# Right operands' sums spread over five value heads, x blocks loaded early, narrow products first

## The reference, cut to what matters

```
Q = x @ Wq ; K = ctx @ Wk ; V = ctx @ Wv          # x: 2 x 2048 x 512, ctx: 2 x 77 x 384, 8 heads of 512
attn = softmax(Q @ K.T / sqrt(512))               # per head, over the 77 keys
out  = concat(attn @ V) @ Wo + x                  # Wo: 4096 x 512
out  = (out - mean) * rsqrt(var + eps) * gamma + beta
```

## Time and profile before

| | us |
|---|---|
| median of 3 runs | 377.33 (377.31 to 377.4) |
| the profiled execution | 378.28 |
| its span, first to last instruction | 376.5 |
| PE busy (2328 matmuls) | 348.5 |
| DVE busy | 295.5 |
| ACT busy | 244.9 |
| POOL busy | 232.1 |

### The profile page before, as it was taken

The page is one execution under the profiler, slowest core; times in us unless marked ns, Lnnn a source line. Parts: engine busy times, 40 slices in busy tenths (PEclk is TensorE's granted clock), DMA queues, the critical chain, the costliest instruction groups (busy, mean ns, idle before and its releaser), DMA issues. The chain is left out here.

```text
span 376.5 us, 7129 instructions
## 1 busy us (share of the span) xinstructions
PE 348.5 (93%) x2328; PEld 316.1 (84%) x2328; DVE 295.5 (78%) x557; ACT 244.9 (65%) x794; POOL 232.1 (62%) x232
## 2 busy tenths in 40 slices
PE   9999999946699963999999999999999999999994
PEld 6999999835588853998998988988989989989984
DVE  2269996799954761689898898898898889889896
ACT  2277556626274561797787697696797697687461
POOL 2046430984274395359878868867877867966233
PEclk9999999996999998699999999999999999999999
DMA  7997678652644301602154143134143234223003
GB/s 243 423 422 286 246 285 310 241 186 86 201 154 166 121 7 52 235 3 96 74 167 141 41 157 139 57 140 141 56 141 141 71 127 143 81 113 109 34 30 111
DMA packets 21348, 56.25 MB, mean 149 GB/s; under 512 B 2560, under 2 KB 4928, under 8 KB 19392
## 3 DMA queue, kind: packets, MB, share of 16 engines
q1 hardware_dynamic: 20448, 54.81, 40.5%
q10 hardware_dynamic: 864, 1.00, 0.9%
HBM read 46.98 MB, written 8.39 MB: 147 GB/s over the span
## 5 line engine op out<-in xcount | busy, mean ns | idle before, releaser
L776 PE MATMUL pair<-vw_hi,pt_hi 128*128 128x512 f32 x155 | 62.2, 401 | 0.0
L776 PE MATMUL pair<-vw_hi,pt_lo 128*128 128x512 f32 x155 | 60.9, 393 | 0.0
L776 PE MATMUL pair<-vw_lo,pt_hi 128*128 128x512 f32 x155 | 60.6, 391 | 0.0
L1466 POOL TENSOR_TENSOR out_sb<-centred,beta_sb 128x512 f32<-128x512 f32 x30 | 38.7, 1290 | 29.0 <-ACT centred L987 29.0
L701 PE MATMUL pair<-a_hi,xo_hi 128*128 128x304 f32 x128 | 40.7, 318 | 9.6 <-DVE u_w L1214 6.1
L942 ACT ACTIVATE prob<-c,neg_max 128x77 f32<-128x77 f32 x128 | 43.9, 346 | 0.0
L1511 POOL TENSOR_TENSOR xo_lo<-x_sum,xo_hi 128x512 fp32r<-128x512 f32 x32 | 41.4, 1298 | 0.0
L701 PE MATMUL pair<-a_lo,xo_hi 128*128 128x304 f32 x128 | 39.3, 307 | 0.0
L701 PE MATMUL pair<-a_hi,xo_lo 128*128 128x304 f32 x128 | 39.3, 307 | 0.0
L980 ACT ACTIVATE pt_hi<-pair 128x640 fp32r<-128x640 f32 x32 | 22.5, 703 | 22.8 <-PE pair L763 22.8
L1299 DVE TENSOR_TENSOR pair<-pair,x_in 128x512 f32<-128x512 f32 x31 | 21.7, 699 | 18.6 <-PE pair L776 16.7
(11 more groups left out here) (141 smaller groups left out, 1066.5 us busy)
## 6 DMA issues: line engine op xcount, KB each, us to landing
w_out<-wo SPq DMA_DIRECT2D x8, 1024.0 KB, 4.8
xt_in<-x_tiles SPq DMA_DIRECT2D x16, 512.0 KB, 4.0
x_in<-x_rows SPq DMA_DIRECT2D x16, 512.0 KB, 4.8
out<-out_sb SPq DMA_DIRECT2D x31, 256.0 KB, 2.2
w_out<-wq_t SPq DMA_DIRECT2D x7, 1024.0 KB, 7.6
w_proj<-wv SPq DMA_DIRECT2D x8, 768.0 KB, 4.9
w_proj<-wk SPq DMA_DIRECT2D x6, 768.0 KB, 9.4
w_out<-wq_t SPq DMA_DIRECT2D x2, 512.0 KB, 7.9
```

Of the source, the lines that this page charges most:

```text
L776: mm = pe.matmul(ps_out[:, i % 2, 0:s.model], ps[:, j, :], v[:, j, b, :], start=(j == 0 and n == 0), stop=(j == s.key_t - 1 and n == len(p ...
L1466: pool.tensor_tensor(out_sb[i % OUT_RING][:, :], centred[i % 2][:, :], beta_sb[:, :], ALU.add)\
```

## The change

- The sums are made in another order (T1, T3, T2, T4, first all of batch 0, then all of batch 1), with two of the four places in PSUM: `sum_z` in `pairs[1]`, `sum_w` in `pairs[3]`. To free these, the value projections' two halves now lie in the two banks of `pairs[0]`, and the main product and the strips have one bank each, in `pairs[2]`. So head h's main product waits for DVE's lo part of head h - 1, and the strips for ACT's copy of head h - 1.
- DVE, ACT: head 8 has T1, T3, T2 of batch 0, head 9 their lo parts and T4, head 10 T4's lo part and T1, T3, T2 of batch 1, head 11 lo parts and T4, head 12 T4's lo part.
- PE: `value_strips(u)` stands ahead of `value_product(u)`. ACT takes the strips ahead of the main product, too.
- `load_xt(0)` is issued in head 10, `load_xt(1)` in head 11.
- The lo part of Wo of head 14 is POOL's instead of DVE's.
- In the main stage ACT's `split_rest` stands ahead of `round_sums(1)`; DVE's `split_rest` stands behind all of the first pair's combining.
- `bias_rows` (the mask's row) and `clear_pad` are earlier.

```diff
-    RESTS_OF_VECTOR = (USES - 2, USES - 1)
+    RESTS_OF_VECTOR = (USES - 1,)
-    T_ORDER = (T1, T2, T3, T4)
-    T_PARTS = [(n, b) for n in T_ORDER for b in range(s.batches)]
+    T_ORDER = (T1, T3, T2, T4)
+    T_PARTS = [(n, b) for b in range(s.batches) for n in T_ORDER]
-        ps_vw = [ps_outp[0][:, n, 0:s.model] for n in range(2)]
-        ps_strips = [ps_outp[1][:, n, 0:P] for n in range(2)]
+        ps_vw, ps_strips = pairs[2][:, 0, 0:s.model], pairs[2][:, 1, 0:P]
+        sum_z, sum_w = pairs[1][:, :, 0:s.kept_half], pairs[3][:, :, 0:s.kept_half]
         def right_steps(b):
-            x, y, z, w = t_tmp[b]
+            x, y, z, w = t_sb[b][:, :, :], t_sb[s.batches][:, :, :], sum_z, sum_w
             return [(z, hi[0][1], lo[0][1], ALU.add), (w, z, hi[0][0], ALU.subtract), (x, w, lo[0][0], ALU.subtract),
-                    (w, hi[1][1], lo[1][1], ALU.add), (y, w, x, ALU.subtract),
-                    (z, w, z, ALU.subtract),
-                    (w, hi[1][0], y, ALU.subtract), (x, w, lo[1][0], ALU.add)]
+                    (y, hi[1][1], lo[1][1], ALU.add), (w, y, z, ALU.subtract),
+                    (z, y, x, ALU.subtract),
+                    (w, hi[1][0], z, ALU.subtract), (x, w, lo[1][0], ALU.add)]
+        def t_sum(n, b):
+            return {T1: t_sb[b][:, :, :], T3: sum_w, T2: sum_z, T4: t_sb[b][:, :, :]}[n]
# SP
-            for c in range(XT_RING):
-                load_xt(c)
+                if H + 2 <= u < H + 2 + XT_RING:
+                    load_xt(u - H - 2)
# PE, value_product and value_strips
-                elif h >= 2:
-                    pe.wait_ge(dve_vw_lo, 2 * (h - 1))
+                else:
+                    pe.wait_ge(dve_vw_lo, 2 * h)
-                if h >= 2:
-                    pe.wait_ge(act_strip, h - 1)
+                if h == 0:
+                    pe.wait_ge(dve_a_lo, 2 * H)
+                else:
+                    pe.wait_ge(act_strip, h)
-                    value_product(u)
-                    value_strips(u)
+                    if u == USES - 1:
+                        open_bank_a()
+                    value_strips(u)
+                    value_product(u)
# ACT
-                if u == H + 1:
-                    for part in T_PARTS[:4]:
-                        round_t(*part)
+                if H < u <= H + 4:
+                    b = (u - H - 1) // 2
+                    if (u - H) % 2:
+                        round_t(T3, b)
+                        round_t(T2, b)
...
+                elif u < USES - 1:
+                    take_strips(u - H)
+                    split_vw(u - H)
+                    if u < H + 4:
+                        round_t(T4 if (u - H) % 2 else T1, (u - H) // 2)
+                else:
                     seed(0)
-                split_vw(u - H)
-                take_strips(u - H)
...
+                    take_strips(u - H)
+                    round_blocks(1)
+                    split_vw(u - H)
             copy_s1(0)
+            split_rest()
             round_sums(1)
-            split_rest()
# DVE
-                if u == H:
-                    right_sum(T1, 0)
+                if u == H + 4:
+                    split_t(T4, 1)
+                elif u < H + 4:
+                    b = (u - H) // 2
+                    if (u - H) % 2:
+                        split_t(T1, b)
+                        split_t(T3, b)
+                        split_t(T2, b)
+                    else:
+                        if b:
+                            split_t(T4, b - 1)
+                        right_sum(T1, b)
                 if u + 1 < USES and by_vector(u + 1):
                     split_w_out(u + 1)
-                if u == USES - 1:
-                    bias_rows()
                 split_vw(u - H)
-                if u == H:
-                    right_sum(T1, 1)
-                    for n in (T2, T3):
-                        for b in range(s.batches):
-                            right_sum(n, b)
...
+                if u < H + 4:
+                    if (u - H) % 2:
+                        right_sum(T4, b)
+                    else:
+                        right_sum(T3, b)
+                        right_sum(T2, b)
+                elif u == H + 4:
+                    bias_rows()
...
-            add_u2(0)
-            split_rest(0)
-            add_w2(0)
+            combine_first(0)
             max_c11(0)
             combine_c22(0)
             combine_c12(0)
             combine_c21(0)
-            split_rest(1)
+            for b in range(s.batches):
+                split_rest(b)
```

More of the change, by code:

```diff
@@ L132, in build @@
             lt("gap1", [P, 256])
-            mask_bias = lt("mask_bias", [P, s.batches, s.half])
-            lt("gap3", [P, P])
+            lt("gap3", [P, s.row + P])
             x_in = [lt(f"x_in{n}", [P, CHUNK, s.model]) for n in range(X_RING)]
@@ L146, in build @@
         with ExitStack() as spare:
-            t_tmp3 = spare.enter_context(nc.sbuf_tensor("t_tmp3", [P, KT, s.kept_half], F32))
+            mask_bias = spare.enter_context(nc.sbuf_tensor("mask_bias", [P, s.batches, s.half], F32))
         rest = [sb(f"rest{n}", [P, 2, s.toks]) for n in range(2)]
@@ L203, in build @@
             with ExitStack() as parts:
-                t_tmp4 = [parts.enter_context(nc.sbuf_tensor(f"t_tmp4_{n}", [P, KT, s.kept_half], F32)) for n in range(3)]
+                second_keys = parts.enter_context(nc.sbuf_tensor("second_keys", [P, s.kept_row], F32))
             wo_lo_late = et("wo_lo_late", [P, s.model_t, s.dim_t, P], F32R)
@@ L311, in second, with keys_at, values_at, whole_proj @@
             return pair[:, :, toks_of(u):2 * toks_of(u)]
+        def keys_at(half):
+            return ps_proj[half][:, :, 0:s.toks]
+        def values_at(half):
+            return pairs[0][:, half, 0:2 * s.toks].rearrange("p (m k) -> p m k", m=2)
+        def whole_proj(u, half):
+            return values_at(half) if u >= H else keys_at(half)[:, :, 0:s.toks if u == 0 else s.kept_toks]
         def ctx_of(u):
@@ L580, in short_product, with full_product @@
                 return mm
-            def full_product(pair, bank, w, moving, m, tiles):
-                toks = moving.shape[2]
+            def full_product(to, w, moving, m, tiles):
                 for k in range(tiles):
-                    mm = pe.matmul(pair[:, bank, 0:toks], w[:, m, k, :], moving[:, k, 0:toks],
+                    mm = pe.matmul(to[:, m % 2, :], w[:, m, k, :], moving[:, k, :],
                                    start=(k == 0), stop=(k == tiles - 1))
@@ L677, in value_product @@
                     for n, (low, w) in enumerate(passes):
-                        mm = pe.matmul(ps_vw[h % 2], values(u, k, low), w[:, k, :], start=(k == 0 and n == 0),
+                        mm = pe.matmul(ps_vw, values(u, k, low), w[:, k, :], start=(k == 0 and n == 0),
                                        stop=(k == s.dim_t - 1 and n == len(passes) - 1))
@@ L1123, in split_kv @@
                     if whole(u):
-                        dve.scalar_tensor_tensor(out=tiles[:, :, toks:2 * toks], in0=first(ps_proj[half], u),
+                        dve.scalar_tensor_tensor(out=tiles[:, :, toks:2 * toks], in0=whole_proj(u, half),
                                                  scalar=kv_scale[u], in1=tiles[:, :, 0:toks].bitcast(F32),
```

89 lines of the change are left out of this document (35 added, 54 removed).

## The result

| | us |
|---|---|
| before, 4 runs | 377.37 (377.31 to 378.49) |
| after, 4 runs | 371.38 (370.9 to 373.41) |
| ratio | 0.9845 [0.9804, 0.9885] |
| profiled execution of after, its span | 370.9, 369.1 |

A forecast was written before the change was run, and what follows sets the result against it. PE, busy 93% of the span, was taken as the bound, with waits to remove. Second pair 7.6 us earlier less 1.6 for the clock, 5.9 taken: 372.4 profiled, median 0.95 below, 371.4; eight in ten 365.5 to 376.

The forecast's parts named there:

- Head 8's wait: On PE, head 8's strips, now leading, wait for POOL's `v_rest` behind Wo's lo part: 2.3 us lost.
- ScalarE's waits for T4: In the value heads, ScalarE's in-order queue waits at L948 for DVE's T4 sum, twice about 5 us.
- The waits at projections 12 and 14: PE waits 2.5 us at each for DVE's lo part, late because ScalarE's rounding waited for T4.
- End of the heads: Value heads end at 134.3 us, gaining 0.9, after 14.3 us of PE waits in ten pieces.
- Strips of heads 11 and 13: On PE, these narrow products were to wait 1.2 us in head 11 and 1.4 us in head 13.
- Rival 3: Heads 11 to 15: the clock falls among small waits and stays down, giving 379.3 us; chance 0.11.
- Sums into PSUM: DVE sums with both inputs in SBUF still take turns with POOL: five turns a batch instead of twelve.
- Rivals 1 and 2: DVE sums: PSUM results free them, 365.7 us, chance 0.14; or all are held and long, 373.7 to 378.1, chance 0.11.
- The strips' chain: Head 14's copy at 128.6, sixteen DMAs end at 141.2, second pair starts at 146.4, 7.6 us earlier.
- The mis-sized term: Behind the second pair's start, all 5.5 us of half clock instead of 2.3: 1.6 us more.
- The sum: At the third pair's first product: 7.6 earlier less 1.6 for the clock, net 6.0 us, taken as 5.9.
- the removal of the 3.5 us wait: Ahead of the score products: with x there early, PE's 3.5 us wait for POOL's lo part goes.

The follow-up runs named there:

- e1: Changed kernel with ScalarE's rounding of T1 and T4 (`round_t`) one head later; 362.98 us, ratio 0.9618 to the kernel before.
- e7: Changed kernel with SP loading both x blocks behind head 13's strips; 376.73 us, ratio 0.9993 to the kernel before.
- e6: Changed kernel with ScalarE copying head 14's strips ahead of the first x block's rounding; 369.06 us, ratio 0.9795 to the kernel before.
- b2: Kernel before with VectorE's two `split_rest` behind all of the first pair's combining, ScalarE's order kept; 376.66 us, ratio 0.9977.
- e3: Changed kernel with both x blocks loaded late, behind the loop over the heads; 372.21 us, ratio 0.9855 to the kernel before.
- b1: Kernel before with the two x blocks loaded inside the loop over the heads, at heads 13 and 14; 375.3 us, ratio 0.9941.
- e2: Changed kernel with the strips' rows split later on ScalarE and VectorE; 370.14 us, ratio 0.9811 to the kernel before.
- e4: Changed kernel with the main product ahead of the narrow ones, on TensorE and ScalarE; 369.6 us, ratio 0.9801 to the kernel before.
- e8: Changed kernel with VectorE making the mask's row (`bias_rows`) in head 15 again, instead of head 12; 373.25 us, ratio 0.9866 to the kernel before.
- c2: Changed kernel with later `round_t` of T1 and T4, late strips' split, third x block ahead of head 15's strips, and main product first; 356.21 us, ratio 0.9462.
- e5: Changed kernel with head 8's `v_rest` ahead of Wo's lo part on GpSimd; 368.95 us, ratio 0.9784 to the kernel before.
- c1: Changed kernel with later `round_t` of T1 and T4, head 8's `v_rest` first, late strips' split, third x block ahead of head 15's strips; 354.88 us, ratio 0.9402.

## Why the prediction was right, step by step

- **Heads 8 to 15.** Head 8's wait: 2.3 predicted, 1.97 measured. ScalarE's waits for T4: about 5 twice, measured 4.95 and 5.30; e1 shows that they are the cause. The waits at projections 12 and 14 (the expectation of e1 calls the first projection 11): 2.5 and 2.5, measured 2.27 and 2.25. End of the heads: 134.3, measured 134.04, of which 0.53 is the start; the gain was to be 0.9 and is 0.6. That the end fits is in part luck: the 14.3 us of losses laid out were all waits, the measured ones are 10.7 us of waits and some 3.3 us by the clock at projections 12 and 14 (from their start to the next product 4.99 and 4.95 us, against 3.32 at the upper clock from 102.34).
- **The small waits were partly the wrong ones.** Strips of heads 11 and 13 were to wait 1.2 and 1.4 us; they do not, because the projection ahead took 1.7 us longer by the clock. That is Rival 3's mechanism at two places, and one sign that the prediction named for being wrong, a clock below 0.9 in heads 11 to 15, did come (0.65 and 0.66 in these two stretches, 0.92 as the mean from 91.21 to 134.04). In head 11 it cost nothing: in e7 the clock stayed up at the same place, PE waited 0.79 us for `v_rest` and 1.71 us for the lo part instead, and the main product began 6.97 us behind the projection, against 6.96 in after. In head 13 `v_rest` is there at 116.62 and the strips begin at 117.75, so about 1 us was lost, an estimate from these two rows. It did not last: Rival 3, a clock that stays down through the heads, fell.
- **Sums into PSUM.** Held or not was decided by the inputs, as assumed:

```profile
69.84 0.80 DVE L1211 TENSOR_TENSOR pair<-pair,a_hi 128x608 f32<-128x608 f32 x1
...
77.91 2.30 DVE L1211 TENSOR_TENSOR pair<-t_sb 128x608 f32<-128x608 f32 x1
...
92.16 2.94 DVE L1211 TENSOR_TENSOR pair<-a_hi,a_lo 128x608 f32<-128x608 f32 x1
```

```profile
70.00 4.73 POOL L1552 TENSOR_TENSOR wo_lo_odd<-w_out,w_out_hi 128x1024 fp32r<-128x1024 f32 x2
...
89.24 5.21 POOL L1552 TENSOR_TENSOR wo_lo_odd<-w_out,w_out_hi 128x1024 fp32r<-128x1024 f32 x2 [5.90 <-ACT w_out_hi L891]
```

  With one input in PSUM the sum takes 0.80 us beside POOL's lo part; with both in SBUF and the result in PSUM (the second and third row) it takes 2.30 and 2.94. The rule of the Trainium skill, page "SBUF — State Buffer", section "SBUF: two separate sides", that the lock goes by "two SBUF inputs", agrees. Rivals 1 and 2 both fall.
- **The strips' chain.** Head 14's copy at 128.6, measured 127.67; moves end at 141.2, measured 140.49; second pair at 146.4, measured 145.59, 8.37 earlier than before where 7.6 were predicted. e6 and e7 move this chain both ways.
- **The mis-sized term** is the clock behind the wait: 1.6 predicted. From the second pair's start to the mark it is 11.48 us before and 12.58 after, so 1.1; b2 gives the same 1.07. The 2.3 us behind 153.96 were right, but the second pair of after does not run 5.5 us at the lower level: its matmuls come every 0.25 us from 145.59 to 150.06 only and then every 0.14, and in half-microsecond steps the clock is at 0.50 from 143.5 on, 2 us ahead of the pair's start. So about 4.5 us of the lower level lie behind the start instead of 5.5.
- **The sum.** 8.37 - 1.10 = 7.27, less 0.53 of the start is 6.7, where 6.0 stood; the medians differ by 6.0. The profiled executions differ by 7.38, since that of before lay 0.9 above its median and that of after 0.5 below. That the median was hit to 0.02 us is luck.
- **A reading to set right.** The prediction calls the clock about half behind each wait of the earlier trace rows. Its first two rows, 0.66 and 0.64, are means over a part at 0.50 and a part at 1.00 (behind the 8.8 us wait it is 0.50 until 91.5 and 1.00 from 92.0). And there was one more such stretch, behind the 3.5 us wait for POOL: in half-microsecond steps the clock is 0.50 from 139.5 to 142.5. It was hidden by the 6.1 us wait that followed, so the sum does not change.
- **What I credited wrongly.** I let the early x load carry the removal of the 3.5 us wait. e3 shows that it isn't needed: in the changed kernel SP reaches the old place of the loads at 119.02 instead of 124.81, as head 12's strips are copied at 112.3 instead of 117.16. Only where SP gets there late (e7, b1) does the order count. b1 and b2 alone bring 2.1 and some 0.8 us. No run has the spread sums, the new banks or the earlier mask's row alone on the kernel before, so how the remaining 3 us are shared stays open.

## What to carry to other kernels

An engine that works in order makes every wait in its queue a wait of all that stands behind: look at the longest waits of the engines that are not the bottleneck, and ask what is behind them. Here moving four roundings by one head each was worth 8.4 us, more than the whole change. And where work is dealt out to remove a long stall, lay the queues out by hand from the trace's durations. It told the gain of the combined edits (354.5 against 354.88) and of e1 (362.4 against 362.98) well. It missed by more in e2 (368.2 against 370.14), where it stopped at the mark, in b1 (374.0 against 375.3), where the mask's row and a longer lower clock were not in it, and in e4 (371.0 at best against 369.6).

## What the hardware showed that was not expected

The granted clock fell behind waits much shorter than the 3.7 us of the earlier trace rows. In the fourteen profiles:

- Behind every wait from 2.97 us up it was at 0.50 for some microseconds.
- Behind waits of 2.25 to 2.28 us it fell thirteen times and once did not (e7, at 93.36, with 24 matmuls in 3.39 us).
- Behind waits of 1.97 us it fell in three executions (e2, e7, e8) and not in four, which is most of the 2.2 us between the two groups.
- Behind waits up to 1.78 us it did not fall (e4, c2), nor behind one of 2.04 us (e2, at 157.29) and one of 2.11 us (b1, at 137.98).

So the length of the wait alone does not decide it near 2 us. Where it fell behind such a wait, it came back within the 24 matmuls that followed (0.50 from 92.5 to 95.5 in after), and those took 1.7 us longer (5.05 against 3.39). The Trainium skill, "TensorE: Matmul & The Clock Gate", section "A second HAM failure mode: psum-queue depth-cycling", says that frequent small idles can make the clock fall and rise; the trace agrees in part: it fell and rose, but behind single waits of about 2 us. A wait of 2 us at PE can therefore cost nearly 4. Taking such waits out also went with steadier times (e5 within 1.2 us, c1 within 0.42), though c2, without head 8's wait, still spreads over 3.2.
